# Rows of Wo made free of their mean on chip: no mean to take off the projection, no shift of x on the scalar engine

## The reference

```
def _layernorm(x, axis=-1, eps=1e-05):
    m = jnp.mean(x, axis=axis, keepdims=True)
    v = jnp.var(x, axis=axis, keepdims=True)
    return (x - m) / jnp.sqrt(v + eps)
...
    qvk = (h @ Wqvk).reshape(b, s, 3, H, HD)          # H = 16 heads of HD = 32
    q, v, k = (qvk[:, :, 0], qvk[:, :, 1], qvk[:, :, 2])
    scores = jnp.einsum('bshi,bthi->bsth', q, k) + causal mask
    weights = jax.nn.softmax(scores / math.sqrt(d), axis=2)
    wv = jnp.einsum('bsth,bthi->bshi', weights, v).reshape(b, s, d)
    return wv @ Wo
...
x = x + _layernorm(attn(_layernorm(x), Wqvk, Wo))
x = x + _layernorm(ffn(_layernorm(x), W1, b1, ..., W2, b2))
```

## Time and profile before

| | us |
|---|---|
| median of 3 runs | 3590.53 (3587.5 to 3594.74) |
| the profiled execution | 3584.82 |
| its span, first to last instruction | 3582.9 |
| mean granted TensorE clock, share of full | 0.956 |

### The profile page before, as it was taken

The page is one execution under the profiler, slowest core; times in us unless marked ns, Lnnn a source line. Parts: engine busy times, 40 slices in busy tenths (PEclk is TensorE's granted clock), DMA queues, the critical chain, the costliest instruction groups (busy, mean ns, idle before and its releaser), DMA issues. The chain is left out here.

```text
span 3582.9 us, 78215 instructions
## 1 busy us (share of the span) xinstructions
PE 3246.1 (91%) x29997; PEld 1878.0 (52%) x29997; DVE 2240.6 (63%) x4221; ACT 2105.8 (59%) x2516; POOL 1333.6 (37%) x766
## 2 busy tenths in 40 slices
PE   6999996989888889889898845999999999999998
PEld 2444442666666666667676722444444444444443
DVE  5444444777676777667676536666666666666665
ACT  2222221988888887979797924445445445445543
POOL 0000001888888897979797920000000000000000
PEclk9999996999999999999999967999999999999999
DMA  3344324122222222222213031000000000000000
GB/s 128 116 134 136 129 102 113 51 66 73 62 85 62 76 70 77 58 85 60 81 56 90 28 111 52 24 24 24 24 23 23 23 23 23 23 23 23 24 24 24
DMA packets 183098, 219.97 MB, mean 61 GB/s; under 512 B 15184, under 2 KB 129936, under 8 KB 182288
## 3 DMA queue, kind: packets, MB, share of 16 engines
q1 hardware_dynamic: 182800, 215.83, 19.1%
HBM read 130.84 MB, written 84.41 MB: 60 GB/s over the span
## 5 line engine op out<-in xcount | busy, mean ns | idle before, releaser
L949 POOL TENSOR_TENSOR a_prob_lo<-a_prob,a_prob_hi 128x2048 f16<-128x2048 f32 (+2 forms) x448 | 1192.1, 2689 | 249.9 <-ACT a_prob_hi L840 247.9
L870 DVE TENSOR_REDUCE a_mx<-a_pw 128x1 f32<-128x512 f32 (+3 forms) x1216 | 753.3, 657 | 165.7 <-PE a_pw L717 122.4
L830 ACT ACTIVATE a_prob<-a_pst,a_lift,a_exp_scale 128x1024 f32<-128x1024 f32 (+1 forms) x640 | 707.3, 1121 | 185.1 <-PE a_pst L770 97.6
L1387 PE MATMUL f_py<-f_w,f_act 128*128 128x512 f16 x3072 | 706.6, 380 | 20.2 <-DVE f_work L1153 12.8
L1377 PE MATMUL f_ph<-f_xT,f_w 128*128 128x512 f16 x3072 | 707.3, 380 | 0.0
L840 ACT ACTIVATE a_prob_hi<-a_prob 128x2048 f16<-128x2048 f32 (+2 forms) x448 | 582.7, 1301 | 0.0
L1325 ACT ACTIVATE f_hidden_work<-f_ph,f_turn,f_fold 128x512 f32<-128x512 f32 x256 | 199.0, 777 | 596.4 <-PE f_ph L1377 595.7
L712 PE MATMUL a_pw<-a_kp,a_qp 96*128 96x512 f16 (+3 forms) x1536 | 469.6, 342 | 75.0 <-DVE a_mx L870 58.4
L1108 POOL TENSOR_TENSOR f_ve<-f_mv,f_eps 128x4 f32<-128x4 f32 x32 | 9.0, 282 | 1384.5 <-DVE f_mv L1134 1384.5
L792 PE MATMUL a_acc<-a_vt,a_prob_hi 128*128 128x33 f16 x9216 | 468.4, 179 | 44.7 <-POOL a_prob_lo L949 24.4
L792 PEld LDWEIGHTS a_acc<-a_vt,a_prob_hi 128*128 128x128 f16 x9216 | 435.9, 97 | 125.3 <-DVE a_o L889 27.9
(11 more groups left out here) (170 smaller groups left out, 3526.0 us busy)
## 6 DMA issues: line engine op xcount, KB each, us to landing
qk_parts<-q_stage SPq DMA_DIRECT2D x128, 256.0 KB, 2.1
a_qp<-qk_parts SPq DMA_DIRECT2D x192, 128.0 KB, 2.6
a_kp<-qk_parts SPq DMA_DIRECT2D x192, 128.0 KB, 2.8
v_parts<-q_vstage SPq DMA_DIRECT2D x16, 1056.0 KB, 5.1
a_vt<-v_parts SPq DMA_DIRECT2D x32, 528.0 KB, 4.4
q_x<-in_L_attn_h_dram SPq DMA_DIRECT2D x16, 1024.0 KB, 7.7
a_xr<-in_L_attn_h_dram SPq DMA_DIRECT2D x64, 256.0 KB, 2.9
x<-a_y SPq DMA_DIRECT2D x64, 256.0 KB, 2.1
```

Source lines behind the costliest of these rows:

```text
L830: act.activation(prob[:, k % PR, :, off:QC], pst[:, k % 2, :, off:QC], ACT.Exp, scale=exp_scale[:, :], bias=lift[:, :]).then_inc(exp_done, 1)
L870: dve.tensor_reduce(out, src, AX_X, ALU.max).then_inc(released, 1)
L949: pool.tensor_tensor(prob_lo[:, first % HR:first % HR + steps, :, off:QC], prob[:, first % PR:first % PR + steps, :, off:QC], prob_hi[:, f ...
L1387: last = pe.matmul(py[:, t, :], act_r[:, f % AR, b, t * P:(t + 1) * P], w2s[:, a, f, :], start=(f == 0 and j == 0), stop=(f == NF - 1 and ...
```

## The change

Taking the mean of the 512 columns off the projection is the same as projecting by a Wo each of whose rows has mean 0. The changed kernel makes Wo such, once, in the prepare block:

- four sums over the rows, one small product by 1/512, four subtractions in place on `a_raw`, and the largest absolute values after that.
- the statistics stay as they are (variance from L904 and L907), but the mean is not used. POOL's third small instruction per tile is gone.
- `shift_x` is gone from ACT. DVE's `wo_out` adds x itself, and waits for POOL's `small_done` and for the load of x, no longer for `x_shifted`.
- `project` emits the same 12 matmuls in the same order and the same halves.

```
+WO_PARTS = 2
+WO_STATS, WO_SMALL, WO_OUT, WO_STORE = 2,2,4,5
...
                 for k in range(KT):
                     dve.wait_ge(w_loaded[k], 16)
-                    then(dve.tensor_reduce(amax[:, k:k + 1], raw[:, k, :], AX_X, ALU.max, apply_absolute_value=True))
+                    last = dve.tensor_reduce(row_mean[:, k:k + 1], raw[:, k, :], AX_X, ALU.add)
+                then(last)
+                then(dve.tensor_scalar(row_mean[:, :], row_mean[:, :], 1 / D, None, ALU.mult))
+                for k in range(KT):
+                    last = dve.tensor_scalar(raw[:, k, :], raw[:, k, :], row_mean[:, k:k + 1], None, ALU.subtract)
+                then(last)
+                for k in range(KT):
+                    last = dve.tensor_reduce(amax[:, k:k + 1], raw[:, k, :], AX_X, ALU.max, apply_absolute_value=True)
+                then(last)
...
-                def shift_x(i, t):
-                    act.wait_ge(small_done, 3 * (QT * i + t) + 3)
-                    act.wait_ge(xr_loaded[t % 2], 16 * (QT // 2 * i + t // 2 + 1))
-                    act.activation(xr[:, t % 2, :], xr[:, t % 2, :], ACT.Identity, bias=small[:, t % YR, 2:3],
-                                   scale=-1.0).then_inc(x_shifted, 1)
...
                 def wo_out(i, t):
                     s, n = t % YR, QT * i + t
-                    dve.wait_ge(x_shifted, n + 1)
+                    dve.wait_ge(small_done, 2 * n + 2)
+                    dve.wait_ge(xr_loaded[t % 2], 16 * (QT // 2 * i + t // 2 + 1))
                     wait(dve, y_stored[s], 16 * (QT // YR * i + t // YR))
                     dve.scalar_tensor_tensor(y[:, s, :], pwo[:, :], small[:, s, 1:2], xr[:, t % 2, :], ALU.mult,
-                                             ALU.subtract
+                                             ALU.add
                                              ).then_inc(y_done, 1)
...
-                    pool.wait_ge(small_done, 3 * n + 2)
-                    pool.tensor_tensor(small[:, s, 2:3], mv[:, s, 0:1], small[:, s, 1:2], ALU.mult
-                                       ).then_inc(small_done, 1)
```

More of the change, by code:

```diff
@@ L385 @@
 WO_AT_LAST = WO_AT
-WO_STATS, WO_SMALL, WO_NORM, WO_OUT, WO_STORE = 2, 2, 3, 4, 5
+WO_PARTS = 2
+WO_STATS, WO_SMALL, WO_OUT, WO_STORE = 2,2,4,5
 assert all(TURN_AT[t // TQ] < at < NS + TURN_AT[t // TQ] for t, at in enumerate(WO_AT))
@@ L488, in attention_phase @@
         amax = sb("amax", [P, KT])
+        row_mean = sb("row_mean", [P, KT])
         top, o_pow2, o_scale, exp_scale = (sb(n, [P, 1]) for n in ("top", "o_pow2", "o_scale", "exp_scale"))
@@ L509, in attention_phase @@
         mv = sb("mv", [P, YR, 2])
-        small = sb("small", [P, YR, 3])
+        small = sb("small", [P, YR, 2])
         half = sb("half", [P, 1])
@@ L532, in attention_phase @@
         xr_loaded = [sem(f"xr_loaded{b}") for b in range(2)]
-        wo_done, x_shifted, y_done = sem("wo_done"), sem("x_shifted"), sem("y_done")
+        wo_done, y_done = sem("wo_done"), sem("y_done")
         y_stored = [sem(f"y_stored{b}") for b in range(YR)]
@@ L574, in _ @@
                 pe.wait_ge(const, 9)
-                pe.wait_ge(vec_step, KT + 1)
+                pe.wait_ge(vec_step, 5)
                 pe.transpose(pw[0:1, 0, 0:P], top[:, :], ident[:, :]).then_inc(top_turned, 1)
-                pe.wait_ge(vec_step, KT + 2)
+                pe.wait_ge(vec_step, 6)
                 pe.matmul(pw[:, 1, 0:2], ones[:, :], top_row[:, :].to_broadcast([1, 2]), start=True, stop=True
@@ L611, in _ @@
             def _(act):
-                act.wait_ge(vec_step, KT + 6)
+                act.wait_ge(vec_step, 10)
                 for k in range(KT):
@@ L739, in shared, with project @@
                     last.then_inc(work_done, 1)
-                def project(i, before, b, t, g, stage):
+                def project(i, before, b, t, part, stage):
                     n = QT * (i + b) + t
-                    if g == 0:
+                    if part == 0:
                         wait(pe, y_done, n)
-                    if g == 0 and t % TQ == 0:
+                    if part == 0 and t % TQ == 0:
                         turn = next((n for n, it in enumerate(stage.work)
@@ L748, in project @@
                         pe.wait_ge(released, before + turn + 1)
-                    for w, a in PASSES:
-                        last = pe.matmul(pwo[:, :], oT[:, a, g, t * P:(t + 1) * P], wo[:, w, g, :],
-                                         start=(g == 0 and (w, a) == PASSES[0]),
-                                         stop=(g == GROUPS - 1 and (w, a) == PASSES[-1]))
-                    if g == GROUPS - 1:
+                    terms = [(g, a, w) for g in range(GROUPS) for w, a in PASSES]
+                    per = len(terms) // WO_PARTS
+                    for j, (g, a, w) in list(enumerate(terms))[part * per:(part + 1) * per]:
+                        last = pe.matmul(pwo[:, :], oT[:, a, g, t * P:(t + 1) * P], wo[:, w, g, :], start=(j == 0),
+                                         stop=(j == len(terms) - 1))
+                    if part == WO_PARTS - 1:
                         last.then_inc(wo_done, 1)
@@ L814, in run @@
                                 shared(i, at, before, what, unit, m, stage)
-                        for part in range(2):
+                        for part in range(WO_PARTS):
                             for b, t in stage.tiles(u, k, part):
-                                for g in range(2 * part, 2 * part + 2):
-                                    project(i, before, b, t, g, stage)
+                                project(i, before, b, t, part, stage)
                 for at, (what, m) in enumerate(AHEAD):
@@ L855, in run @@
                             high(i, *e)
-                        for b, t in stage.tiles(u, k, WO_NORM):
-                            shift_x(i + b, t)
                 run_all(act, run)
```

2 lines of the change are left out of this document (1 added, 1 removed).

## The result

| | us | against the kernel before |
|---|---|---|
| changed kernel, median of 4 runs | 3526.72 (3525.57 to 3528.13) | 0.9821 [0.9804, 0.9838] |
| kernel before, median of 4 runs beside it | 3590.98 (3587.5 to 3594.74) | |
| span of the profiled execution | 3524.9 (before 3582.9) | |
| mean granted clock | 0.966 (before 0.956) | |

The change gives 64 us, not 35.

The account below looks back on a forecast made before the run. Where tiles are, PE's work and its gaps were taken to set the pace. Waits -20, clock -10, drain -5.7, prepare block +1.2 gave -34.5, rounded -35: from 3590.5 to 3555 us, range 3527 to 3578.

Parts of the forecast that it names:

- The waits in the loop: Attention loop: DVE no longer waits for POOL's third product and ACT's shift; 2.6 us per batch, taken as 20 us.
- Tile 4's gap: PE's idle gap at tile 4 of the loop: falls from 1.75 to some 0.65 us, 1.1 us.
- the loop's turn: PE's 4.04 us gap at tile 1, at the end of the loop's turn: stays, so tile 1 gives 0.
- The pair of tiles: Tiles 4 and 5 of the loop together: 1.5 us, with tile 5's power 0.6 us earlier.
- The clock: PE's granted clock behind tile 0's gap: 1.7 us in seven batches at 0.8, 10 us; tile 5's not counted; bounds 0 and 24.
- not in unit 2: Sign in the profile after: unit windows shrink in units 3, 0 and 1, but unit 2's does not.
- The drain: Tiles 2 to 7 of the last batch: DVE starts earlier behind POOL's power, 5.7 us saved for six tiles; clock left at 0.
- The prepare block: Added sums, small product and subtractions on DVE, mostly beside SP's loads: 1.2 us added, bounds 0 and 2.
- A: Rival: more gain; all idle time less the turn goes, 35 us, clock gives 24, with drain and block -63, to 3527; chance 0.22.
- B: Rival: hidden anyway; ACT's and POOL's chain paces, PE's gaps only move; -4.5, to 3586; chance 0.12.
- C: Rival: slower; PE's gap per tile pair becomes several, more followed by 1.2 GHz; +23, to 3613; chance 0.08.

Follow-up runs that it names:

- e1: Changed kernel, but ACT again waits for POOL's small values and does an unused activation per tile, for which DVE does not wait: 3539.8 us.
- e5: Changed kernel with ACT free, DVE made late by two unused row sums at tiles 0, 1, 4, 5 and in the drain: 3561.25 us.
- e4: Kernel before the change, with unused matmuls on PE in the gaps behind tiles 0, 4 and 5: 3560.79 us.
- e10: Changed kernel with an idle ACT shift that DVE waits for, and POOL's third small product, for which ACT waits, put back: 3585.28 us.
- e13: e10 with unused matmuls on PE in the gaps behind tiles 0, 4 and 5: 3559.8 us.
- e3: Changed kernel, but in the drain alone ACT does an idle activation behind POOL's value and DVE waits for it: 3532.77 us.
- e7: Changed kernel with two PSUM tiles in turn for the projections of the drain: 3511.3 us.
- e8: Changed kernel with Wo left as loaded, without the removal of the rows' mean in the prepare block: 3532.37 us.
- e15: Changed kernel with POOL's third small product back and DVE waiting for it, ACT free: 3544.21 us.
- e6: Changed kernel with POOL's small values made ahead of that step's low part: 3515.74 us.
- e12: Changed kernel with POOL's small values ahead of the low part, two PSUM tiles in the drain, and DVE's last product a step earlier: 3529.15 us.

## Why the prediction was wrong

**The waits in the loop: right.** 20 us forecast, 20.5 of PE's idle time gone. Tile 4's gap fell by 1.0 us (1.1 forecast), tile 5's by 1.0, the loop's turn stayed. The total is partly luck. The pair of tiles gave 2.0 and not 1.5 us: ACT's exponential behind tile 4 came 2.4 us earlier against POOL's power and not 0.6, since its scores were there at 1377.4 (those that end near 1379.3 belong to the next exponential). Tile 5's power came 1.0 us earlier and not 0.6. The three windows with tiles lost 3.3 us of idle time a turn for 2.6 forecast, and unit 2's grew by 0.3. That ACT's relief acts through POOL at tile 5 is seen in the rounding that comes earlier, and in e1's gap of 1.69 us there. e5 against e1 (34.5 us and 13) shows that DVE was the larger part, as the chain was read.

**The clock: this step failed.** I counted one stretch of 1.7 us a turn at 0.8, 10 us, with 24 as the upper bound. Measured: 27.4 us less busy time in the loop for the same matmuls. For tile 0 that was right: 6 stretches went, for 5.6 counted. But I left tile 5's at nothing, because its gap would remain at 1.5 us or more. It remains with 1.47 us, and 6 of its 7 stretches went. Tile 4's 2 went as well. And 6 went in unit 2, which lost 0.9 us of busy time a turn, where I had said "not in unit 2". These 14 stretches were not in the sum. The fillers of e4 show the term by itself, 26 us without any wait removed, and e10 and e13 (25.5 us apart) show it again. In the prediction the loss was priced at two gaps that I had looked at; the trace held 38 such stretches in the loop, and that sum, 64.8 us, was there to be read. But unit 2's 6 stretches, 10 us, could not be read from any gap: the one there is 1.20 to 1.22 us in every run, and the clock fell behind it in 1 to 7 of 7 turns. It is no mere scatter of one execution, for the loops of e3 and e7, which are that of the changed kernel, have 18 stretches too, 1 and 3 of them in unit 2. What decides it is not shown.

**The drain: mis-sized.** 5.7 us forecast. The wait fell by 1.03 us per tile, close to the 0.95 taken, but the five periods from tile 2 to tile 7 shrank by 9.1 us, 1.8 each. The rest is the clock again, which I had put at 0: the matmuls of the five periods took 4.0 us less, and before the last tile's twelve took 5.30 us. e3 gives back 6.0 us (7.2 in its profile) of the drain's gain without the third product.

**The prepare block: near.** +1.2 forecast, +0.2 by PE's first piece (e8 allows 0.7). The four subtractions took 1.77 us, not 2.2, and the block stayed SP's.

**The rivals.** A's number came out, for partly other reasons: it had all idle time less the turn go (35 us), and 20.5 went; it had 24 for the clock, and it was 27 with more in the drain. So its number is luck. B is refuted by the unit windows, each of them shorter. C, more drops of the clock, is refuted by 18 for 38, but its mechanism is real: in e15 a delay of 0.28 us brings 7 more stretches and 9.7 of the loop's 15.0 us.

**Open.** What decides which gap is followed by 1.2 GHz. Length alone does not: the gaps of 1.20 and 1.22 us above had one of each outcome, and unit 2's gap, the same in all runs, had both. Tile 5's gap was followed by a stretch in 5 of 7 turns at 1.69 us (e1), and in only 1 both at 1.47 (the changed kernel) and at 2.3 (e5). So I can count the stretches that went, but not say how many a given edit will save. Nor is it shown why DVE starts later at tile 0 in e8.

## What to carry to other kernels

Where the granted clock falls behind short gaps of the matrix engine, add up the lost clock over the whole stretch first and take it as a term as large as the waits, with a wide range; here 0.28 us per tile was worth 12 us with the gaps filled and 33 without. Look for an in-order engine that waits late in front of work which frees a PSUM bank, and move what it waits for ahead on the producer (e6), not the wait itself (e12). In a tail with a single accumulator, a second tile from idle PSUM halves it (e7).
